# Token placement split between VectorE and GpSimd, first convolution taps moved to ScalarE and GpSimd, in a fused Mamba and mixture-of-experts layer

## The chip, the core and the metric

The kernel runs on one core of a Trainium2 chip. The time is that of one execution on the device, in microseconds (us); the median of several runs is given. A second figure is the span of one profiled execution, from its first to its last instruction.

The engines are called as in the profile: PE (TensorE, matmul; PEld is its weight load), DVE (VectorE), ACT (ScalarE), POOL (GpSimd), SP (SyncE, which issues most DMAs). Each has a queue of its own and works it off in order. They meet only at semaphores.

## What is computed

For x of shape 8 x 512 x 256 (batch, time, channels), with everything in float32:

```python
xn = layernorm(x)
# Mamba branch, per batch of 512 steps
x_ssm, x_gate = split(xn @ in_proj_w.T + in_proj_b)
x_conv = silu(causal_conv_4_taps(x_ssm) + conv_b)
B, C = split(x_conv @ bc_w.T + bc_b)            # 16 states
dt = softplus(x_conv @ dt_w.T + dt_b)
h = h * exp(dt * -exp(A_log)) + dt * B * x_conv   # over time, each channel and state
y = (sum over states of h * C + x_conv * D) * silu(x_gate)
mamba = layernorm(y @ out_w.T + out_b + xn) * ln_g + ln_b
# expert branch, on all 4096 tokens
logits = silu(xn @ rw1 + rb1) @ rw2 + rb2         # 8 experts, the best 2 are taken
w = softmax over the two taken logits
moe = xn + sum over the two of w * (silu(xn @ we1[e] + be1[e]) @ we2[e] + be2[e])
out = x + mamba + moe
```

## The kernel before

**Stage one** (to about 71 us) normalises x, transposes it, computes the router's logits and writes xn to scratch memory. **Stage two** begins with a block that runs once, and then has a loop over 8 batches of 9 steps. In each step PE computes one tile of 128 tokens through one expert (`up`, `down`), ACT applies Silu and the weights, POOL gathers a later tile's tokens and scatters this one's results with indirect DMAs, and DVE runs two of the 16 states of the Mamba scan: `times_b` (L947), `scan` (L954), `times_c` (L961). ACT makes the decay factors for the scan (`decay`, L778) and POOL adds up y (L598). A switch between Silu and Exp costs ACT a table load each time (L805). 71 steps carry an expert tile.

**The block that runs once** is what matters here. DVE first does the routing arithmetic (L1031 to L1081) on small tables of 128 x 256 and less, about 40 instructions, nearly each waiting for the one before (`link`): the best two experts of each token, and for each of the 2 x 4096 pairs a slot number, split in a tile number `af` (0 to 73) and a position `bf` in the tile. `idv` is the token id of a pair and `wv` its softmax weight. ACT gives an exponential for it (L883, waited for by L1079).

Then the ids and weights are **placed** in tables by matmul, in 8 chunks of 8 slots a lane each (`NCH`, `CH`). For a chunk:
- DVE makes a one-hot of the tile number, `oa` (one instruction, L1088, 8 x 74 elements a lane), and one of the position, `ob` (L1093, 8 x 128 elements).
- POOL multiplies oa by the ids (`ids_in`, L664), ACT multiplies it by the weights in 8 activations (`weights_in`, L795). The two halves form `ov`.
- PE adds ob^T x ov to the table in PSUM (`place`, L1307, 8 matmuls).

All is double-buffered: a chunk waits until the matmuls of the last but one are done (`s_placed`). The first batch's convolution stands between: ACT makes x_ssm and the first tap (`conv_in`, L697, L706), DVE adds the other three taps for each half of the channels (`tap`, L928, a fused multiply-add of 512 elements), three after chunk 1 and three after chunk 3. DVE also counts which expert each tile has (L1105 to L1108, `te_i`). PE does the matmuls for B, C and the step sizes (`first`, L1320) before chunk 4, ACT reads them (`first_bc`, `first_dt`), SP stores B and C, which are then loaded back once for each state, spread to all lanes (`rep`).

Last, DVE copies the placed table out of PSUM: `sid` (scatter ids), `wslot` (weights), `gid` (gather ids), L1115 to L1117. The gather of the first tile waits for that, then PE transposes it (`turn_x`, L1228), ACT copies it (`copy_x`, L785), and `up` begins. ACT meanwhile does exp and ln for the step size (L755, L759), the first decays and y's start (`start_sum`, L769). The **gate** projection of batch 0 (PE L1179, ACT L713) stands in steps 0 and 1 of the loop. SP loads the next batch's xn (`load_xnt`, L508) only when that projection has been done, and the loads of rep (L544) stand behind it in SP's queue.

## Time and profile before

| | |
|---|---|
| median of 3 runs | 923.11 us (922.67 to 924.55) |
| the profiled execution, its time | 921.83 us |
| the profiled execution, its span | 919.7 us |
| busy over the span | PE 85%, DVE 85%, ACT 72%, POOL 65% |
| mean granted TensorE clock | 0.962 of full speed |

The profile lists the busy time of each engine, groups of equal instructions with what ended the idle time before them, and the chain of work that ended last. A share of busy time is an average over very different stages, so the stretch from 71 to 160 us is read in its own timeline.

### The profile page before, as it was taken

To read this page: it belongs to the slowest core of one execution; us is meant where nothing else is said; L and a number is where in the kernel's file an instruction comes from. 1 tells how busy PE (TensorE), PEld (TensorE's weight loads), DVE (VectorE), ACT (ScalarE), POOL (GpSimd) and SP (SyncE) were. 2 spreads that over 40 slices of the span, in tenths; PEclk is the share of its full clock that TensorE was granted. 3 is DMA by queue.
4 is the path that set the end of the run, shared out by engine and by line. 5 is a ranking of instruction groups with operands and counts; after the bars stand their busy time and mean duration, and the time that the engine had idled before them with its cause. 6 is when DMAs were issued, how large, how long until landed. Compare 5 with 4: busy or idle time off the path is not lost.

```text
span 919.7 us, 14382 instructions
## 1 busy us (share of the span) xinstructions
PE 785.5 (85%) x4533; PEld 631.8 (69%) x4533; DVE 783.9 (85%) x774; ACT 663.4 (72%) x1134; POOL 599.1 (65%) x384
## 2 busy tenths in 40 slices
PE   3994959988999899898998899989889998999942
PEld 2661747867777778677876777677768776778831
DVE  6817947999989978997899889989899889989993
ACT  1433678878689768976897869887888778869920
POOL 3570425767577757776678847885688477758861
PEclk9995879999999999999999999999999999999986
DMA  9949536667577856787658866785678586977541
GB/s 286 390 167 294 200 144 230 200 202 244 189 238 209 253 191 226 208 260 238 223 184 247 275 182 213 224 286 172 222 212 276 180 256 196 265 226 235 186 91 24
DMA packets 81928, 201.02 MB, mean 219 GB/s; under 512 B 7936, under 2 KB 41216, under 8 KB 81728
## 3 DMA queue, kind: packets, MB, share of 16 engines
q1 hardware_dynamic: 61424, 171.46, 53.4%
q0 software_dynamic: 19168, 26.59, 15.2%
q10 hardware_dynamic: 1264, 2.05, 0.7%
q8 instruction: 40, 0.66, 0.3%
q14 instruction: 32, 0.26, 0.1%
HBM read 174.38 MB, written 26.61 MB: 219 GB/s over the span
## 4 chain that ended last, share of the span: by engine, by line
DVE 30%; PE 23%; ACT 14%; DMA 11%; issue 11%; POOL 3%; DVEq 0%; ACTq 0%; POOLq 0%; SPq 0%
DVE ps_drive L954 11%; PE ps_up L1248 9%; DVE ring L961 7%; DMA out<-yo,sid 6%; DVE ps_drive L947 6%; PE ps_yx L1262 5%; PE ps_fr L1179 4%; ACT L805 4%; ACT da L778 3%; DMA out<-xtok 3%; DVE xx L928 2%; DMA bc_scratch<-sp 1%; PE ps_fr L1204 1%; PE ps_up L1242 1%; POOL y L598 1%
## 5 line engine op out<-in xcount | busy, mean ns | idle before, releaser
L598 POOL TENSOR_TENSOR y<-y,ring 128x1024 f32<-128x1024 f32 x126 | 323.0, 2563 | 65.6 <-ACT y L769 52.5
L954 DVE TENSOR_TENSOR_SCAN ps_drive<-da,ps_drive 128x1024 f32<-128x1024 f32 x128 | 293.7, 2295 | 37.3 <-ACT da L778 33.6
L1248 PEld LDWEIGHTS ps_up<-xgt,w1s 128*128 128x128 f32 x2272 | 280.5, 194 | 18.2 <-issue 9.9
L1248 PE MATMUL ps_up<-xgt,w1s 128*128 128x128 f32 x2272 | 280.0, 277 | 0.0
L1262 PE MATMUL ps_yx<-w,ht 128*128 x1136 | 272.7, 384 | 0.0
L1262 PEld LDWEIGHTS ps_yx<-w,ht 128*128 128x128 f32 x1136 | 207.7, 193 | 29.2 <-issue 5.0
L587 POOL DMA_INDIRECT out<-yo,sid x71 | 116.4, 1639 | 128.3 <-ACT yo L820 99.2
L805 ACT ACT_TABLE_LOAD x143 | 183.5, 1283 | 2.5
L947 DVE TENSOR_TENSOR ps_drive<-ps_u,rep 128x1024 f32<-128x1024 f32 x128 | 157.3, 1229 | 25.0 <-DMA rep<-bc_scratch 16.2
L778 ACT ACTIVATE da<-gd,col 128x511 f32<-128x511 f32 x256 | 168.3, 710 | 0.0
L961 DVE TENSOR_TENSOR ring<-ps_drive,rep 128x1024 f32<-128x1024 f32 x128 | 156.6, 1223 | 3.9
L812 ACT ACTIVATE ht<-ps_up 128x512 f32<-128x512 f32 x142 | 80.7, 587 | 74.6 <-PE ps_up L1248 74.3
L1179 PE MATMUL ps_fr<-xx,wm 128*128 128x512 f32 (+1 forms) x212 | 104.9, 618 | 17.2 <-ACT sp L740 12.7
L578 POOL DMA_INDIRECT xg<-xn_scratch,gid x71 | 72.8, 1025 | 30.5 <-PE ps_up L1228 13.3
L1242 PE MATMUL ps_up<-sel,bpart 96*128 96x512 bf16 x142 | 55.3, 390 | 27.3 <-ACT xgt L785 26.1
L1179 PEld LDWEIGHTS ps_fr<-xx,wm 128*128 128x128 f32 (+1 forms) x212 | 35.5, 185 | 47.8 <-issue 32.2
L820 ACT ACTIVATE yo<-ps_yx,wslot 128x256 f32<-128x256 f32 x71 | 33.0, 464 | 40.5 <-DMA out<-yo,sid 31.5
L928 DVE SCALAR_TENSOR_TENSOR xx<-xs,col,xx 128x512 f32<-128x512 f32 x48 | 52.3, 1090 | 9.9 <-ACT xx L706 9.2
L1242 PEld LDWEIGHTS ps_up<-sel,bpart 96*128 x142 | 14.0, 99 | 55.3 <-issue 54.4
L1228 PE MATMUL ps_up<-ident,xg 128*128 128x128 f32 x142 | 27.9, 279 | 18.7 <-ACT ht L812 9.9
L1228 PEld LDWEIGHTS ps_up<-ident,xg 128*128 128x128 f32 x142 | 19.3, 142 | 28.3 <-issue 22.0
L237 POOL TENSOR_TENSOR w<-w,da 128x1024 f32<-128x1024 f32 x8 | 18.8, 2351 | 23.0 <-DVE da L288 14.1
(172 smaller groups left out, 710.5 us busy)
## 6 DMA issues: line engine op xcount, KB each, us to landing
w1s<-in_we SPq DMA_DIRECT2D x71, 1024.0 KB, 7.4
rep<-bc_scratch SPq DMA_DIRECT2D x128, 512.0 KB, 4.8
w<-in_we SPq DMA_DIRECT2D x8, 1024.0 KB, 12.0
w<-in_x SPq DMA_DIRECT2D x8, 512.0 KB, 11.2
xn_scratch<-da SPq DMA_DIRECT2D x8, 512.0 KB, 7.1
out<-w POOLq DMA_DIRECT2D x8, 512.0 KB, 6.5
xnt_scratch<-xx SPq DMA_DIRECT2D x8, 512.0 KB, 5.6
xx<-xnt_scratch SPq DMA_DIRECT2D x8, 512.0 KB, 3.2
```

What stands on the lines that cost most here:

```text
L587: pool.indirect_dma_start(out[:, :], bass.IndirectOffsetOnAxis(ap=sid[:, s:s + 1], axis=0), yo[:, :], None, bounds_check=TOK - 1, oob_is_e ...
L598: pool.tensor_tensor(y[:, :, :], y[:, :, :], ring[:, g % RING, :, :], ALU.add).then_inc(s_sum, 1)
L778: act.activation(da[:, g % DECAYS, k, 1:], dtt[:, k, 1:], ACT.Exp, scale=aneg[:, k, n:n + 1]).then_inc(s_decay, 1)
L805: act.activation(scrap[:, n % 4:n % 4 + 1], col[:, 0:1], func).then_inc(s_table, 1)
L812: act.activation(ht[:, j % HBUF, 4 * h:4 * h + 4, :], psum[f"up{h}"][:, :].rearrange("p (k c) -> p k c", c=P), ACT.Silu).then_inc(s_hidden, 1)
L947: dve.tensor_tensor(drive[:, :, :], u[:, :, :], rep[:, g % REPS, 0:1, :].to_broadcast([P, KD, L]), ALU.mult).then_inc(s_times_b, 1)
L954: dve.tensor_tensor_scan(states, da[:, g % DECAYS, :, :].rearrange("p k l -> p (k l)"), states, 0.0, ALU.mult, ALU.add).then_inc(s_scanned, 1)
L961: dve.tensor_tensor(ring[:, g % RING, :, :], drive[:, :, :], rep[:, g % REPS, 1:2, :].to_broadcast([P, KD, L]), ALU.mult).then_inc(s_times ...
L1179: mm = pe.matmul(psum["fr"][0:rows_out, :], wm[:, k, at:at + rows_out], src[:, k, :], start=(k == 0), stop=(k == KD - 1))
L1242: pe.matmul(bank[:, :], bup[:, bass.ds(e, 1), :], sel[:, 4 * h:4 * h + 4].unsqueeze(2).to_broadcast([PARTS, 4, P]), start=True, stop=False)
L1248: mm = pe.matmul(bank[:, c * P:(c + 1) * P], w1s[:, q, k, at:at + P], xgt[:, k, :], start=False, stop=(c == 3 and k == KD - 1))
L1262: mm = pe.matmul(yx_y, ht[:, j % HBUF, k, :], w2[:, bass.ds(e, 1), k, :], start=False, stop=(k == KH - 1))
```

## The change

- `oa` is gone. DVE writes the id half of ov directly: 8 instructions a chunk, each `(k_j == af) * idv` for one slot column (74 elements), then ob as before. POOL writes the weight half likewise with 8 instructions a chunk. ACT has no part in it any more. DVE and POOL no longer wait for each other, only for `s_placed`. Both buffers of ov now lie in `da`.
- First taps: ACT computes the six products (three per half, `products_of`), POOL adds them to xc (`first_taps`). DVE does all one-hots without taps between.
- The gate projection of batch 0 moves from the loop's steps 0 and 1 to just before the placements (PE) and behind the taps' products (ACT).
- PE's matmuls for B, C and step sizes move from before chunk 4 to behind the last chunk, and what ACT does with them with it. copy_x(0) moves ahead of ln_dt, and the first Silu of the experts ahead of the first decays. Three decays instead of two are made then.
- `gid` is written first, and the gather waits for it alone.

```diff
-        pair = [a.rearrange("p b k l -> p (b k l)") for a in (da[:, 0:2, :, :], gd[:, :, :, :])]
-        oa = [a[:, 2 * CH * MC:3 * CH * MC].rearrange("p (a c) -> p a c", c=MC) for a in pair]
-        ov = [a[:, 0:2 * CH * MC].rearrange("p (a v c) -> p a v c", v=2, c=MC) for a in pair]
+        placed = da.rearrange("p b k l -> p (b k l)")
+        ov = [placed[:, q * 2 * CH * MC:(q + 1) * 2 * CH * MC].rearrange("p (a v c) -> p a v c", v=2, c=MC)
+              for q in range(2)]
+        products = [a[:, k, :] for a in (ring[:, 2, :, :], ring[:, 3, :, :], da[:, 3, :, :]) for k in range(KD)]
...
-        uses = [("in", 0, 0), ("in", 0, 1)]
+        uses = [("in", 0, 0), ("in", 0, 1), ("gate", 0, 0), ("gate", 0, 1)]
...
                 def gather(j):
-                    pool.wait_ge(s_tables, 2)
+                    pool.wait_ge(s_tables, 1)
...
-                def ids_in(n):
+                def first_taps(m):
+                    pool.wait_ge(s_tap0, m + 1)
+                    for t in range(1, TAPS):
+                        if t > 1:
+                            pool.wait_ge(s_taps, (TAPS - 1) * m + t - 1)
+                        at = (TAPS - 1) * m + t
+                        pool.wait_ge(s_products, at)
+                        pool.tensor_tensor(xc[:, m, :], xc[:, m, :], products[at - 1], ALU.add).then_inc(s_taps, 1)
+
+                def weights_in(n):
                     q = n % 2
-                    pool.wait_ge(s_values, 1)
                     if n > 1:
                         pool.wait_ge(s_placed, n - 1)
-                    pool.wait_ge(s_tile_onehot, n + 1)
-                    pool.tensor_tensor(ov[q][:, :, 0, :], oa[q],
-                                       idv[:, bass.ts(n, CH)].unsqueeze(2).to_broadcast([P, CH, MC]),
-                                       ALU.mult).then_inc(s_ids_in, 1)
+                    for c in range(CH):
+                        at = n * CH + c
+                        ins = pool.tensor_scalar(ov[q][:, c, 1, :], k_j, af[:, at:at + 1], wv[:, at:at + 1],
+                                                 ALU.is_equal, ALU.mult)
+                    ins.then_inc(s_weights_in, 1)
...
-                    for c in range(CH):
-                        at = n * CH + c
-                        act.activation(ov[q][:, c, 1, :], oa[q][:, c, :], ACT.Copy,
-                                       scale=wv[:, at:at + 1]).then_inc(s_weights_in, 1)
...
+                def products_of(m):
+                    for t in range(1, TAPS):
+                        w = C_CW + TAPS * m + t
+                        act.activation(products[(TAPS - 1) * m + t - 1], xs[:, m, t:t + L], ACT.Copy,
+                                       scale=col[:, w:w + 1]).then_inc(s_products, 1)
...
-                for n in range(NCH):
-                    if n == 4:
-                        conv_act(0)
-                    if n == 5:
-                        first_bc()
-                    weights_in(n)
+                for m in range(KD):
+                    gate_in(0, m, front["gate", 0, m])
+                conv_act(0)
+                first_bc()
                 for m in range(KD):
                     first_dt(m)
                 exp_dt(0)
+                copy_x(0)
                 ln_dt(0)
-                copy_x(0)
-                table_of(ACT.Exp)
-                act.wait_ge(s_a, 2)
-                for r in range(NU):
-                    decay(0, 0, r)
-
-                start_sum(0)
                 table_of(ACT.Silu)
                 for h in range(2):
                     hidden(0, h)
                 copy_x(1)
                 table_of(ACT.Exp)
+                act.wait_ge(s_a, 2)
+                for r in range(NU):
+                    decay(0, 0, r)
+                decay(0, 1, 0)
+                start_sum(0)
...
                     if n > 1:
-                        dve.wait_ge(s_ids_in, n - 1)
-                        dve.wait_ge(s_weights_in, (n - 1) * CH)
-                    dve.tensor_tensor(oa[q], k_j.unsqueeze(1).to_broadcast([P, CH, MC]),
-                                      af[:, bass.ts(n, CH)].unsqueeze(2).to_broadcast([P, CH, MC]),
-                                      ALU.is_equal).then_inc(s_tile_onehot, 1)
-                    if n > 1:
                         dve.wait_ge(s_placed, n - 1)
+                    for c in range(CH):
+                        at = n * CH + c
+                        ins = dve.tensor_scalar(ov[q][:, c, 0, :], k_j, af[:, at:at + 1], idv[:, at:at + 1],
+                                                ALU.is_equal, ALU.mult)
+                    ins.then_inc(s_ids_in, 1)
...
-                for m in range(KD):
-                    for n in (2 * m, 2 * m + 1):
-                        one_hot(n)
-                    for t in range(1, TAPS):
-                        tap(0, m, t)
+                for n in range(3):
+                    one_hot(n)
...
                 proj_in(0, 1, 1)
+                for m in range(KD):
+                    proj_in(0, KD + m, front["gate", 0, m])
...
                 for n in range(NCH):
-                    if n == 4:
-                        pe.wait_ge(s_conv, KD)
-                        first(FIRST[0], W_BC, NBC)
-                        for m in range(KD):
-                            first(FIRST[m + 1], W_DT + m * P, P)
                     chunk(n)
+                pe.wait_ge(s_conv, KD)
+                first(FIRST[0], W_BC, NBC)
+                for m in range(KD):
+                    first(FIRST[m + 1], W_DT + m * P, P)
```

The queue of DVE at the start of the placements, before (`da` and `gd` hold oa and ov of the two buffers, `ring` holds ob, `rep` the small tables, `xx` the convolution):

```order
L1081 TENSOR_TENSOR rep<-rep 128x32 [waits s_link]
L1088 TENSOR_TENSOR da<-rep 128x592 [waits s_xn_stored1,s_xn_stored0]
L1093 TENSOR_TENSOR ring<-rep 128x1024
L1088 TENSOR_TENSOR gd<-rep 128x592
L1093 TENSOR_TENSOR ring<-rep 128x1024
L928 SCALAR_TENSOR_TENSOR xx<-xs,col,xx 128x512 [waits s_tap0]
L928 SCALAR_TENSOR_TENSOR xx<-xs,col,xx 128x512 [waits s_taps] x2
L1088 TENSOR_TENSOR da<-rep 128x592 [waits s_weights_in,s_ids_in]
L1093 TENSOR_TENSOR ring<-rep 128x1024 [waits s_placed]
```

and after the change (the line numbers are those of the changed kernel):

```order
L1089 TENSOR_TENSOR rep<-rep 128x32 [waits s_link]
L1097 TENSOR_SCALAR da<-rep 128x74 [waits s_xn_stored1,s_xn_stored0]
L1097 TENSOR_SCALAR da<-rep 128x74 x7
L1100 TENSOR_TENSOR ring<-rep 128x1024
L1097 TENSOR_SCALAR da<-rep 128x74 x8
L1100 TENSOR_TENSOR ring<-rep 128x1024
L1097 TENSOR_SCALAR da<-rep 128x74 [waits s_placed]
L1097 TENSOR_SCALAR da<-rep 128x74 x7
L1100 TENSOR_TENSOR ring<-rep 128x1024
```

Each wide oa became eight narrow instructions, the taps left this queue, and the only wait for another engine is the one for PE's earlier matmuls.

The queue of POOL at the same place, before (behind the branch comes stage two):

```order
L572 UNCONDITIONAL_BRANCH [waits barrier_Pool_Activation_PE_DVE_SP_gather]
L664 TENSOR_TENSOR da<-da,rep 128x8x74 [waits s_tile_onehot,s_values]
L664 TENSOR_TENSOR gd<-gd,rep 128x8x74 [waits s_tile_onehot,s_values]
L664 TENSOR_TENSOR da<-da,rep 128x8x74 [waits s_tile_onehot,s_placed,s_values]
L664 TENSOR_TENSOR gd<-gd,rep 128x8x74 [waits s_tile_onehot,s_placed,s_values]
```

and after:

```order
L573 UNCONDITIONAL_BRANCH [waits barrier_Pool_Activation_PE_DVE_SP_gather]
L666 TENSOR_TENSOR xx<-xx,ring 128x512 [waits s_products,s_tap0]
L666 TENSOR_TENSOR xx<-xx,ring 128x512 [waits s_products,s_taps] x2
L666 TENSOR_TENSOR xx<-xx,ring 128x512 [waits s_products,s_tap0]
L666 TENSOR_TENSOR xx<-xx,da 128x512 [waits s_products,s_taps] x2
L674 ISA
L674 TENSOR_SCALAR da<-rep 128x74 [waits s_values,s_xn_stored1,s_xn_stored0]
L674 TENSOR_SCALAR da<-rep 128x74 x15
L674 TENSOR_SCALAR da<-rep 128x74 [waits s_placed]
L674 TENSOR_SCALAR da<-rep 128x74 x7
```

Six additions now run while DVE is still at the routing arithmetic, and 64 short instructions stand where 8 wide ones stood.

## Rows read from the trace of the kernel before

**Rows 1.** The page: each engine's busy time, share of the span and instructions.

```profile
PE 785.5 (85%) x4533; PEld 631.8 (69%) x4533; DVE 783.9 (85%) x774; ACT 663.4 (72%) x1134; POOL 599.1 (65%) x384
```

**Rows 2.** The chain that ended last, in order: start, duration, engine and line.

```profile
81.97 0.18 DVE rep L1054
...
89.03 0.77 DVE da L1088
89.80 1.14 DVE ring L1093
90.94 1.66 DVE gd L1088
...
121.58 0.21 DVE gid L1117
...
184.77 1.23 DVE ps_drive L947
...
220.50 2.31 DVE ps_drive L954
```

**Rows 3.** Timeline of the placements: start, duration, engine, line, operation, [idle before].

```profile
89.95 2.02 POOL L664 TENSOR_TENSOR da<-da,rep 128x592 f32<-128x592 f32 x1 [23.57 <-DVE da L1088]
90.85 1.75 DVE L1088 TENSOR_TENSOR gd<-rep 128x592 f32<-128x592 f32 x1
...
92.12 4.28 PE L1307 MATMUL ps_up<-da,ring 128*128 128x148 f32 x16 [7.95 <-ACT da L795]
...
118.73 2.25 PE L1307 MATMUL ps_up<-gd,ring 128*128 128x148 f32 x16 [0.62 <-ACT gd L795]
```

**Rows 4.** Timeline of DVE and POOL near 46 us, from narrow windows.

```profile
45.71 1.05 DVE L288 TENSOR_SCALAR da<-w,sp 128x256 f32<-128x256 f32 x3
...
46.67 2.44 DVE L288 TENSOR_SCALAR da<-w,sp 128x256 f32<-128x256 f32 x1
...
46.59 2.38 POOL L237 TENSOR_TENSOR w<-w,da 128x1024 f32<-128x1024 f32 x1 [2.75 <-DVE da L288]
```

**Rows 5.** Groups of instructions: count | busy us, mean ns of one | idle before.

```profile
L257 POOL TENSOR_TENSOR w<-w,bpart 96x1024 f32<-96x1024 f32 x1 | 2.1, 2121 | 0.1
...
L609 POOL TENSOR_SCALAR mv<-mv 128x4 f32<-128x4 f32 x7 | 1.6, 224 | 0.6 <-issue 0.2
...
L256 POOL CAST bpart<-w 96x1024 bf16<-96x1024 f32 x1 | 1.0, 1033 | 0.1
...
L257 POOL TENSOR_TENSOR w<-w,bpart 96x256 f32<-96x256 f32 x1 | 0.7, 667 | 0.1
...
L256 POOL CAST bpart<-w 96x256 bf16<-96x256 f32 x1 | 0.4, 392 | 0.1
...
L769 ACT ACTIVATE y<-xx,col 128x512 f32<-128x512 f32 x16 | 10.6, 711 | 0.0
...
L928 DVE SCALAR_TENSOR_TENSOR xx<-xs,col,xx 128x512 f32<-128x512 f32 x48 | 52.3, 1090 | 9.9 <-ACT xx L706 9.2
```

**Rows 6.** Busy us of PE, PEld, DVE, ACT, POOL; PE clock, DMA share, GB/s.

```profile
71.40:89.00 17.60, 7.77 (x10) 2.53 (x10) 13.99 (x40) 4.63 (x7) 0.00 (x0) 0.60 1.00 325
```

**Rows 7.** Timeline behind the placements.

```profile
129.68 0.66 PE L1228 MATMUL ps_up<-ident,xg 128*128 128x128 f32 x2 [8.70 <-DMA xg<-xn_scratch,gid]
...
133.60 2.30 DVE L954 TENSOR_TENSOR_SCAN ps_drive<-da,ps_drive 128x1024 f32<-128x1024 f32 x1 [4.20 <-ACT da L778]
...
137.37 1.06 ACT L812 ACTIVATE ht<-ps_up 128x512 f32<-128x512 f32 x2
```

**Rows 8.** Timeline of the first steps, DVE and SP's queue.

```profile
148.79 2.30 DVE L954 TENSOR_TENSOR_SCAN ps_drive<-da,ps_drive 128x1024 f32<-128x1024 f32 x1 [0.45 <-ACT da L778]
...
152.51 0.96 SPq L544 DMA_DIRECT2D rep<-bc_scratch  x2
...
161.03 1.23 DVE L947 TENSOR_TENSOR ps_drive<-ps_u,rep 128x1024 f32<-128x1024 f32 x1 [3.76 <-DMA rep<-bc_scratch]
...
166.14 1.88 DVE L928 SCALAR_TENSOR_TENSOR xx<-xs,col,xx 128x512 f32<-128x512 f32 x1 [1.55 <-ACT xx L706]
```

More of the change, by code:

```diff
@@ L493, in build @@
                 uses.append(("out", b - 1, 1))
-            uses += [("gate", b, 0), ("gate", b, 1)]
+                uses += [("gate", b, 0), ("gate", b, 1)]
             if b < B - 1:
@@ L838, in step @@
                     prepare = b < B - 1
-                    if i + 1 < IN:
+                    if i + 1 < IN and s > 0:
                         decay(b, i + 1, 0)
@@ L846, in step @@
                             hidden(s + 1, h)
-                    if i in (0, 1):
+                    if i in (0, 1) and b > 0:
                         gate_in(b, i, front["gate", b, i])
@@ L1108, in _ @@
                 dve.tensor_scalar(te_i[:, :], wslot[:, :], -1.0, None, ALU.add).then_inc(s_expert, 1)
-                for n in range(4, NCH):
+                for n in range(3, NCH):
                     one_hot(n)
@@ L1114, in _ @@
                 dve.wait_ge(s_expert, 1)
+                dve.tensor_scalar(gid[:, :], ids, k_pad, float(TOK - 1), ALU.add, ALU.min).then_inc(s_tables, 1)
                 link(dve.tensor_scalar(sid[:, :], ids, k_pad, None, ALU.add))
                 dve.tensor_copy(wslot[:, :], psum["up0"][:, MC:2 * MC]).then_inc(s_tables, 1)
-                dve.tensor_scalar(gid[:, :], ids, k_pad, float(TOK - 1), ALU.add, ALU.min).then_inc(s_tables, 1)
                 for r in range(DECAYS):
@@ L1282, in step @@
                     e_after = expert(s + 2) if s + 2 < MT else None
-                    if i == 0:
+                    if i == 0 and b > 0:
                         proj_in(b, KD, front["gate", b, 0])
@@ L1291, in step @@
                         down(s, e, 1)
-                    if i == 0:
+                    if i == 0 and b > 0:
                         proj_in(b, KD + 1, front["gate", b, 1])
@@ L1312, in chunk @@
                     pe.wait_ge(s_ids_in, n + 1)
[L1313 removed]
+                    pe.wait_ge(s_weights_in, n + 1)
                     for a in range(CH):
@@ L1324, in _ @@
                 for n in range(NCH):
[L1325 to L1329 removed]
                     chunk(n)
+                pe.wait_ge(s_conv, KD)
+                first(FIRST[0], W_BC, NBC)
+                for m in range(KD):
+                    first(FIRST[m + 1], W_DT + m * P, P)
                 pe.wait_ge(s_first_read, 3)
+                pe.wait_ge(s_tables, 2)
                 turn_x(0)
[L1334 removed]
                 e = expert(0)
```

19 lines of the change are left out of this document (8 added, 11 removed).

## The prediction, made before the changed kernel ran

> **What bounds the kernel now.** I read the page first: no engine is the bound over the whole span, PE and DVE are both busy for 85% of it and ACT for 72% [rows 1]. The change leaves the loop over 71 expert steps as it was and rewrites what stands between the routing arithmetic and the first step, about 80 to 150 us. So I followed the chain of waits there. It runs on DVE through the routing arithmetic to 89.0 us, on through the one-hots and taps (L1088, L1093, L928), to the last placement matmuls, the table gid at 121.6 [rows 2], then the gather, a transpose and ACT's table loads and decays. What moves the end of this stage moves the kernel: from 184.8 to 222.8 the chain is DVE work with no gap, five steps of multiply, scan, multiply [rows 2]. A delay of VectorE by then is a delay of the end.
>
> Two marks serve for the sum: T, when the pair weights are ready and the one-hots start (89.03), and E, when the last placement matmul ends (118.73 + 2.25 = 120.98) [rows 3].
>
> The timeline of 89 to 93 us shows what paces the placements. The first oa of DVE takes 0.77 us, the next 1.75. POOL's multiply began at 89.95 and ended at 91.97; the second oa has 592 elements, 0.62 us at the pace of its neighbours (1024 elements in 1.14 us with the step to the next), and 91.97 + 0.62 is just its end, 92.60 [rows 2, 3]. So VectorE waited until GpSimd was through, and GpSimd (2.02 us for 1.30 us of work, below) had waited for ob before that. The two engines take turns at SBUF. One chunk then costs 2.80 us (89.80 to 92.60) [rows 2], and ACT's eight activations hide behind it.
>
> **Does that hold for a tensor_scalar?** It is the form that the change puts on both engines. At 46.67 an L288 (256 elements) started while POOL ran from 46.59 to 48.97; it took 2.44 us and ended at 49.11, 0.14 after POOL [rows 4]. Undisturbed, three take 1.05 us with 0.41 for the last one, so they start 0.32 apart [rows 4]. It does wait for GpSimd, and of its 0.32 us only 0.14 is streaming, 0.185 is fixed.
>
> The Trainium skill says the same of the port (SBUF — State Buffer, "Who interferes with whom": the pair is an exclusive lock, tensor_scalar can take it, and so does a VectorE instruction with two SBUF inputs against a reading GpSimd one); the traces agree. It speaks against this change, which puts both engines on short instructions of that kind.
>
> **Part 1, taps to ACT and POOL.** Removed from DVE: six L928, at their mean of 1.09 us (waits for POOL in it) 6.5 us of the chain [rows 5]. Added on ACT: six Copy with scale, 0.71 us each as L769 [rows 5], in a stretch where ACT is busy 4.63 of 17.6 us [rows 6]. The exp of the logit difference moves behind them, to about 87.9; DVE asks for it some 0.7 us before T, so nothing is lost there, the less if DVE is late.
> Added on POOL: six additions of 512 elements. POOL's two-input price is 667 ns for 256 and 2121 for 1024 elements, so 1.89 ns each on 0.18 fixed [rows 5]: 1.15 us each, 6.9 us, from the first product (81.5) to about 91. POOL was idle there (0.00 busy) [rows 6], but the routing chain of DVE was not: from 81.97 to 89.03 it is about twenty linked instructions, nearly all with two SBUF inputs or of the copy and tensor_scalar kind [rows 2]. I walked both queues against each other, each waiting for the other's running instruction: the links at L1054, L1056, L1060, both L1066 and the first cast are held for about 0.7, 1.2, 0.4, 1.0, 0.4 and 0.4 us; the two reductions and the links with a PSUM input pass. That is **T later by 4.0 us** (bounds 0, if such short instructions slip between, and 6.9, every addition in full).
>
> **Part 2, the placements.** VectorE: eight TENSOR_SCALAR of 74 elements in place of one oa. By the above 0.185 + 0.04 = 0.23 us apart [rows 4], 1.84 a chunk, plus 1.14 for ob: 2.98. (Bounds 0.04, streaming alone, and 0.32, the 256-element step.) GpSimd: 224 ns for four elements (L609), plus 70 elements at 0.83 ns (the casts, 1033 and 392 ns) gives 0.28 us, 2.26 a chunk [rows 5]. No row has a compare with column operands on GpSimd: bounds 0.22, that row alone, and 0.45, twice its fixed part. While ob streams, POOL's reads are held [rows 3], so its chunk is 2.26 + 1.14 = 3.40, and DVE's eight, taking turns with POOL's eight, come to the same. I take **3.40 us a chunk**, against 2.80 now (bounds 2.25, PE's own chunk [rows 3], and 5.2 = 8 x (0.23 + 0.28) + 1.14 if nothing overlaps).
>
> The Trainium skill has another price for VectorE (VectorE: DVE Perf Modes, the section on the TRN2 errata: 58 cycles plus the elements over the speed-up, at 0.96 GHz). An estimate from that page is 0.10 us for each of the eight and 1.93 us a chunk, below PE's; by it the sum below would end about 9 us lower (8 x (3.40 - 2.25), since PE then sets the pace), if GpSimd kept up.
>
> PE: the two gate projections now stand before chunk 0. They take the clock of that stretch (0.60) [rows 6], 3.6 us each with ACT's Silu table and the first gate between, until about 93.6; ob(0) is ready at 96.4, so they are covered. Their cover is thin only if T doesn't move. Chunk 0 takes 4.1 us at the low clock (the row's 4.28 laps over into the next) [rows 3], placed at 100.5, while DVE, which no longer has taps to fill with, wants buffer 0 at 99.8: 0.7 us of wait. The expert table (L1105 to L1108) stays, 1.74 us.
> Sum: T = 89.03 + 4.0 = 93.0; + 8 x 3.40 = 27.2; + 0.7 + 1.7; + 2.25 for the last chunk: E = 124.9. **Against 120.98 that is 3.9 later.**
>
> **Part 3, behind E.** The matmuls for B, C and the step sizes (5.7 us) come after the chunks, so do their ACT reads, the store of B and C, exp and ln. On SP the bc store now precedes the rep loads directly. gid first saves 0.5 us of the gather, which is covered: ACT is at exp_dt until E + 9.2, and only then copies x, at E + 9.6 (now E + 9.4, behind the transpose) [rows 7]. Then ln (with its table), Silu table, hidden(0), copy_x(1), Exp table, decays. PE has worked until E + 5.6 instead of idling 8.70 us [rows 7], so I take the first up at the high clock, hidden(0) done at E + 15 instead of E + 17.45 (138.43) [rows 7]. The first scan then starts at E + 18.1, now E + 12.6 [rows 7]: **VectorE is 5.5 us later there**. But behind it three waits stood: 0.45 for a decay, 3.76 for a rep transfer, 1.55 for the next conv_in [rows 8]. The second comes from SP: load_xnt waits for the second gate projection of step 1, and rep, issued at 152.51, queues behind it [rows 8]. With the gates early, that is gone. PE loses 2 x 1.9 us of projections in step 0 and is about 2 us ahead at step 3. So VectorE ends up 5.5 - 5.8 = **0.4 earlier** (the other end: cold PE, scan at E + 20.2, 1.6 later).
>
> **Sum:** 3.9 - 0.4 = +3.5. The profiled execution would have 919.7 + 3.5 = 923.2 span and 925.3 time. The median of the runs shown is 1.3 above the profiled time: **926.6 us**.
>
> **Rivals.**
> (a) The port doesn't bite: each instruction holds it so briefly (0.04 of 0.23 us) that both streams slip through. T stays, chunks take 2.98: chunk 0 waits for the gates until 93.6 and is placed at 97.7; 97.7 + 3.0 + 1.7 + 14.9 + 2.25 = 119.6, 1.4 earlier, with the tail 1.8: 921.3. At PE's pace of 2.25 a chunk: 97.7 + 2.25 + 1.7 + 11.25 + 2.25 = 115.2, 916.9. For it: POOL's start at 46.59 fell between two instructions of DVE and cost POOL nothing visible (2.38 us for 1024 elements, by the price above 2.12) [rows 4, 5]. Against it: the 0.62 and 0.14 behind POOL's end. It wins as long as T stays and a chunk is under 3.3 us (97.7 + 6 x 3.3 + 1.7 + 2.25 = 121.4 is today's E plus what the tail gives). Chance 0.26.
> (b) GpSimd's compare is slow, or nothing overlaps. At 0.40 us each, 8 x 0.40 + 1.14 = 4.34 a chunk: 93 + 34.7 + 1 + 2.25 = 131, 933. Fully serial 5.2: 93 + 41.6 + 1.7 + 2.25 = 138.6, +17.2, 940. It passes the forecast once an instruction on GpSimd costs over 0.33. For it: two column operands and a compare, seen in no row. Chance 0.17.
> (c) The start's shift is swallowed by later waits in the loop (of the kind of the 1.55 for conv_in) [rows 8]: 923.1. Against it: the gapless DVE chain from 184.8. Chance 0.07.
> The forecast's own case, 3.1 to 3.8 us a chunk with T 3 to 6 later, gives E 0.8 to 8.7 later and 923.5 to 931. Chance 0.50.
>
> **How the numbers follow.** A measurement of this kernel can tell about 0.2%, 1.8 us, from no change. (a) is faster but for its slow edge; (c) and the low edge of the forecast are the same; the rest is slower: faster 0.25, same 0.14, slower 0.61. The range leaves out the fast end of (a) and the serial end of (b): 918 to 937; the forecast alone has 923.5 to 931.
>
> **What the profile after would show.** Right: DVE's routing links at 82 to 91 us longer than 0.42, T near 93; one-hots 3.4 us apart with ob blocking POOL; E near 125; first scan 18 us behind E; no rep wait near 160. Wrong, to the fast side: links still 0.17 to 0.42 and T near 89, or VectorE's eight in under 1.2 us. Wrong, to the slow side: GpSimd's instruction over 0.35 us, PE waiting for the weights before each chunk. If E is as forecast but the end is not, the tail is what I mis-sized.

## The result, and the profile after

The changed kernel takes 950.11 us (median of 6 runs, 945.89 to 951.33), the kernel before 923.43 (6 runs beside it, 920.87 to 925.20): a ratio of 1.0282, 95% interval 1.0254 to 1.0310. I had forecast 926.6 with a range of 918 to 937. The sign was right, the size was not: the loss is 26.7 us where I had 3.5, and the range ended 13 us too early. Here and below a median is over all runs of a kernel, while a ratio leaves out the few runs that lie over 1.5% above the fastest of their kernel.

The page of the profiled execution (949.45 us, span 947.7), the rows that answer [rows 1] and three groups of instructions:

```profile
PE 798.2 (84%) x4533; PEld 640.2 (68%) x4533; DVE 790.4 (83%) x824; ACT 649.0 (68%) x1074; POOL 641.5 (68%) x446
...
DVE 28%; PE 20%; ACT 16%; DMA 11%; issue 9%; POOL 7%; SPq 0%; DVEq 0%; ACTq 0%; POOLq 0%
...
L674 POOL TENSOR_SCALAR da<-rep 128x74 f32<-128x74 f32 x64 | 48.3, 773 | 3.4 <-DVE rep L1089 3.4
L1313 PE MATMUL ps_up<-da,ring 128*128 128x148 f32 x128 | 26.3, 380 | 26.3 <-POOL da L674 26.3
```

POOL is 42 us busier than before, and 48.3 of its microseconds are the 64 instructions that make the pair weights, 773 ns each. My sum had 280 for one by itself and 425 with VectorE's wide compare spread over the eight of a chunk (3.40 / 8). POOL's share of the chain that ended last is 7%, where it was 3%. PE's last column says the rest: in all 26.3 us of its waits within the placements it waited for POOL, and for nobody else.

The timeline of the stage, POOL first, then PE, then DVE (start, duration, engine, line, operation, [idle before and its releaser]). These rows stand against [rows 2, 3]:

```profile
79.72 5.27 POOL L666 TENSOR_TENSOR xx<-xx,ring 128x512 f32<-128x512 f32 x4 [14.19 <-ACT ring L886]
85.07 2.74 POOL L666 TENSOR_TENSOR xx<-xx,da 128x512 f32<-128x512 f32 x2
91.18 48.27 POOL L674 TENSOR_SCALAR da<-rep 128x74 f32<-128x74 f32 x64 [3.37 <-DVE rep L1089]
```

```profile
86.29 3.48 PE L1183 MATMUL ps_fr<-xx,wm 128*128 128x512 f32 x4 [2.88 <-ACT gd L727]
98.17 4.29 PE L1313 MATMUL ps_up<-da,ring 128*128 128x148 f32 x16 [8.40 <-POOL da L674]
...
134.84 4.29 PE L1313 MATMUL ps_up<-da,ring 128*128 128x148 f32 x16 [5.29 <-POOL da L674]
139.60 2.71 PE L1313 MATMUL ps_up<-da,ring 128*128 128x148 f32 x16 [0.47 <-POOL da L674]
```

```profile
79.87 1.40 DVE L1064 TENSOR_TENSOR ht<-rep 128x256 f32<-128x256 f32 x1
...
81.90 0.54 DVE L1068 TENSOR_TENSOR_SCAN rep<-rep 128x8 f32<-128x8 f32 x1
...
82.67 1.13 DVE L1070 TENSOR_SCALAR rep<-rep 128x8 f32<-128x8 f32 x1
...
84.29 0.98 DVE L1072 TENSOR_TENSOR xtok<-xtok,rep 128x256 f32<-128x256 f32 x1
85.31 1.37 DVE L1074 TENSOR_TENSOR ht<-y,xtok 128x256 f32<-128x256 f32 x1
...
87.34 0.75 DVE L1074 TENSOR_TENSOR ht<-xtok 128x256 f32<-128x256 f32 x1
...
90.87 1.93 DVE L1097 TENSOR_SCALAR da<-rep 128x74 f32<-128x74 f32 x8
92.72 1.26 DVE L1100 TENSOR_TENSOR ring<-rep 128x1024 f32<-128x1024 f32 x1
...
102.50 2.03 DVE L1097 TENSOR_SCALAR da<-rep 128x74 f32<-128x74 f32 x8 [5.56 <-PE ps_up L1313]
```

How to read them. POOL's third row is one unbroken stretch: from 91.18 to 139.45 it never waits, 48.27 / 8 = 6.03 us a chunk. Everything else in the stage waits for it: PE before every chunk, DVE for a buffer that PE could not free (5.56 us at 102.50). DVE's eight narrow instructions take 1.93 us, 0.23 apart, as forecast. Before that stretch, six routing links stand out: 1.40, 0.54, 1.13, 0.98, 1.37 and 0.75 us. They lie beside POOL's six additions (79.72 to 87.81). The same six in the kernel before:

```profile
82.18 0.42 DVE L1056 TENSOR_TENSOR ht<-rep 128x256 f32<-128x256 f32 x1
...
83.22 0.17 DVE L1060 TENSOR_TENSOR_SCAN rep<-rep 128x8 f32<-128x8 f32 x1
...
83.63 0.17 DVE L1062 TENSOR_SCALAR rep<-rep 128x8 f32<-128x8 f32 x1
...
84.29 0.43 DVE L1064 TENSOR_TENSOR xtok<-xtok,rep 128x256 f32<-128x256 f32 x1
84.75 0.42 DVE L1066 TENSOR_TENSOR ht<-y,xtok 128x256 f32<-128x256 f32 x1
...
85.84 0.43 DVE L1066 TENSOR_TENSOR ht<-xtok 128x256 f32<-128x256 f32 x1
```

The stage by marks. S is where stage two starts (the memset of xs: 71.45 before, 69.13 after; stage one is the same code, and its 2.3 us are spread). T is the start of the first one-hot, E the end of the last placement matmul (139.60 + 2.71 = 142.31).

| | before | after | difference |
|---|---|---|---|
| S | 71.45 | 69.13 | -2.3 |
| S to T | 17.58 | 21.74 | +4.2 |
| T to E | 31.95 | 51.44 | +19.5 |
| E to the end of the span | 798.7 | 805.4 | +6.7 |
| span | 919.7 | 947.7 | +28.0 |

### The profile page after: what moved, and what is told of

The parts are those of the page before. It is cut to its first block, busy times and chain, and to the rows that moved or that the text cites. A ratio compares the mean times of both kernels' runs of the same rounds, so it can differ in the third digit from the quotient of the medians.

```text
span 947.7 us, 14419 instructions
## 1 busy us (share of the span) xinstructions
PE 798.2 (84%) x4533; PEld 640.2 (68%) x4533; DVE 790.4 (83%) x824; ACT 649.0 (68%) x1074; POOL 641.5 (68%) x446
## 4 chain that ended last, share of the span: by engine, by line
DVE 28%; PE 20%; ACT 16%; DMA 11%; issue 9%; POOL 7%; SPq 0%; DVEq 0%; ACTq 0%; POOLq 0%
DVE ps_drive L962 11%; DMA out<-yo,sid 8%; PE ps_up L1252 7%; DVE ring L969 6%; DVE ps_drive L955 6%; POOL da L674 5%; ACT L808 4%; PE ps_fr L1183 4%; ACT da L792 3%; PE ps_yx L1266 3%; PE ps_fr L1208 2%; DMA bc_scratch<-sp 2%; DVE xx L936 1%; DMA rep<-bc_scratch 1%; ACT ht L815 1%
## 5 line engine op out<-in xcount | busy, mean ns | idle before, releaser
L1252 PEld LDWEIGHTS ps_up<-xgt,w1s 128*128 128x128 f32 x2272 | 283.9, 196 | 17.7 <-issue 9.4
L1252 PE MATMUL ps_up<-xgt,w1s 128*128 128x128 f32 x2272 | 283.5, 279 | 0.0
L1183 PE MATMUL ps_fr<-xx,wm 128*128 128x512 f32 (+1 forms) x212 | 108.5, 636 | 25.4 <-ACT sp L754 16.6
L936 DVE SCALAR_TENSOR_TENSOR xx<-xs,col,xx 128x512 f32<-128x512 f32 x42 | 44.8, 1068 | 8.6 <-ACT xx L720 8.1
L674 POOL TENSOR_SCALAR da<-rep 128x74 f32<-128x74 f32 x64 | 48.3, 773 | 3.4 <-DVE rep L1089 3.4
L1313 PE MATMUL ps_up<-da,ring 128*128 128x148 f32 x128 | 26.3, 380 | 26.3 <-POOL da L674 26.3
L1313 PEld LDWEIGHTS ps_up<-da,ring 128*128 128x128 f32 x128 | 24.3, 265 | 29.3 <-issue 29.3
```

The lines of the kernel that those rows point to most:

```text
L674: ins = pool.tensor_scalar(ov[q][:, c, 1, :], k_j, af[:, at:at + 1], wv[:, at:at + 1], ALU.is_equal, ALU.mult)
L1183: mm = pe.matmul(psum["fr"][0:rows_out, :], wm[:, k, at:at + rows_out], src[:, k, :], start=(k == 0), stop=(k == KD - 1))
L1252: mm = pe.matmul(bank[:, c * P:(c + 1) * P], w1s[:, q, k, at:at + P], xgt[:, k, :], start=False, stop=(c == 3 and k == KD - 1))
```

## The experiments

Each ratio is to runs of the kernel before that were taken beside the run; their medians are 923.4 to 924.3 us.

**The disputed cost by itself.** To the end of the kernel before I added a row of instructions on POOL that write tiles nobody reads any more: the form of the change, and the same with one property taken away at a time; then the form again beside VectorE's narrow and wide ones.

```diff
+for r in range(6):
+    pool.tensor_scalar(spot(MC), src, c1, c2, ALU.is_equal, ALU.mult)   # then mult, mult; constants; 8 and 592 elements
+for r in range(8):                          # once beside 24 narrow ones on VectorE, once beside 4 wide compares
+    ins = pool.tensor_scalar(spot(MC), src, c1, c2, ALU.is_equal, ALU.mult)
```

> The kernel before, with a tail of instructions on idle engines that write unused tiles (the output isn't touched). GpSimd alone, 74 elements a lane: six tensor_scalar with is_equal and mult by columns, six mult and mult by columns, six is_equal and mult by constants, six mult and mult by constants, six with one mult by a constant, six with is_equal and mult by columns on 8 elements, two of them on 592. Then eight of the first form with VectorE working at 24 tensor_scalar of 74, and eight with VectorE working at 4 is_equal of 1024 elements (two SBUF inputs). Theory P (price): the form itself costs about 0.60 us on idle GpSimd, and mult by constants about 0.28, so the price sits in the columns or in the compare; 592 elements would then be about 1.0. Theory L (turns at the port): alone the form costs 0.28, and 0.6 to 0.77 only with VectorE beside it. Both: beside the wide VectorE instruction an instruction of GpSimd takes 1.4 to 1.5, since that one holds the port for 1.1 us.

The timeline of POOL and DVE there:

```profile
922.91 3.63 POOL L701 TENSOR_SCALAR ring<-gam,col 128x74 f32<-128x74 f32 x6 [4.09 <-DMA out<-xtok]
926.53 2.36 POOL L703 TENSOR_SCALAR ring<-gam,col 128x74 f32<-128x74 f32 x6
928.87 2.60 POOL L705 TENSOR_SCALAR ring<-gam 128x74 f32<-128x74 f32 x6
931.43 1.36 POOL L707 TENSOR_SCALAR ring<-gam 128x74 f32<-128x74 f32 x6
...
934.96 2.32 POOL L711 TENSOR_SCALAR ring<-gam,col 128x8 f32<-128x8 f32 x6
937.27 4.66 POOL L713 TENSOR_SCALAR ring<-da,col 128x592 f32<-128x592 f32 x2
...
942.64 5.38 POOL L718 TENSOR_SCALAR ring<-gam,col 128x74 f32<-128x74 f32 x8
942.58 5.58 DVE L1217 TENSOR_SCALAR xx<-gam,col 128x74 f32<-128x74 f32 x24 [26.81 <-POOL da L715]
...
949.04 8.67 POOL L725 TENSOR_SCALAR ring<-gam,col 128x74 f32<-128x74 f32 x8
948.98 2.36 DVE L1222 TENSOR_TENSOR gd<-gam 128x1024 f32<-128x1024 f32 x2 [0.82 <-POOL da L722]
```

Divide each row by its count. Compare and multiply by two columns (L701): 0.604 us. Without the compare (L703): 0.393. With constants in place of columns (L705): 0.433. With neither (L707): 0.227, somewhat less than my estimate of 0.28. So the columns cost 0.17 and the compare 0.21, and neither was in my price. Between 8 and 74 elements (0.387 and 0.604) the form goes by 3.3 ns an element, and two of 592 took 2.33 us each, where I had expected about 1.0. Beside 24 narrow instructions of VectorE it takes 5.38 / 8 = 0.67, 0.07 more; beside four wide compares 8.67 us for eight, (8.67 - 8 x 0.604) / 4 = 0.96 us for each wide one. VectorE itself lost nothing beside it: 5.58 / 24 = 0.23, and 1.22 us for a wide compare.

That makes the stage: 64 x 0.604 = 38.7, plus 8 x 0.96 = 7.7 for the eight wide compares of ob, is 46.3 of the 48.27 us. The other 1.9 us is of the size of the turns beside the narrow ones (64 x 0.07 would be 4.5 if all stood beside one). The changed kernel's own trace has the same price. At 95.89 VectorE runs ob, from 98.60 it is idle; the last line, of another view, is for all 64 (shortest, median and longest in ns):

```profile
95.89 1.54 POOL L674 TENSOR_SCALAR da<-rep 128x74 f32<-128x74 f32 x1
...
98.60 2.40 POOL L674 TENSOR_SCALAR da<-rep 128x74 f32<-128x74 f32 x4
...
L674 POOL TENSOR_SCALAR da<-rep x64: 611/615/2157, 91.2 to 138.8; 128x74 f32<-128x74 f32 x64
```

With nothing beside it an instruction takes 2.40 / 4 = 0.60 us; the one beside ob takes 0.9 more. The longest, 2.16 us, stood beside ob and the compare of the expert table behind it.

**The change in its parts.** First everything but the placements; then the taps alone; then the rest of the tail alone.

```diff
 # everything but the placements (e2): as after, but ids and weights as before
-ins = pool.tensor_scalar(ov[q][:, c, 1, :], k_j, af[:, at:at + 1], wv[:, at:at + 1], ALU.is_equal, ALU.mult)
+pool.tensor_tensor(ov[q][:, :, 0, :], oa[q], idv[:, bass.ts(n, CH)]..., ALU.mult)      # and ScalarE's eight weights
```

> The changed kernel with the placements as before: wide one-hot on VectorE, one wide multiply on GpSimd, eight activations on ScalarE; taps, gates ahead and the matmuls behind stay as changed. Theory P: the placements carry 20 to 25 us of the 26.7, the chunks go back to 2.8 us, E to about 3 to 5 later than before by the taps' 4.1, the time to 926 to 931. Theory L gives the same here. A rival, that the loss sits in the order behind the placements (cold clock of TensorE, decays late), leaves over 10 us: 935 or more.

> The kernel before, with the first taps alone moved to ScalarE and GpSimd; all else as before. Port theory: the routing arithmetic on VectorE ends 4.1 us later (the six additions hold the port), and the six fused taps, 6.2 us between the chunks, are gone from VectorE; the chunks are then paced by turns at the port, 2.8 each: E about 1 earlier to 1 later, time 921 to 925. If the port doesn't matter for the arithmetic, T stays and the time is 918 to 920.

> The kernel before, with the order around the placements alone changed: first gate projections ahead, matmuls for B, C and step sizes behind the last chunk, their ScalarE work with it, gid first; both buffers of the one-hots in one tile. My prediction's step: E 2 earlier or equal (the six matmuls, 5.7 us, leave the middle, where they stood before chunk 4), the first scan at E + 18 to 20 instead of E + 12.6, no wait for rep near 160: 0.4 earlier to 1.6 later behind E, time 920 to 925. If the late first scan isn't absorbed by the missing waits, 926 to 930.

Everything but the placements: 925.35 us, ratio 0.9993 (0.9961 to 1.0025). Taps alone: 925.73, 1.0012 (0.9983 to 1.0041). Gates ahead, B, C and step sizes behind: 927.43, 1.0037 (1.0011 to 1.0063). From the ratio 0.9993 to 1.0282 is 2.9%, about 26.7 us, with some 3 us of doubt: **the placements carry the whole loss** within that. The other two parts together can't be told from no change, though the tail alone costs 0.37%, clear of noise by little. The first one-hot of the three, in this order (S at 70.24, 69.22 and 68.74):

```profile
91.58 0.77 DVE L1111 TENSOR_TENSOR da<-rep 128x592 f32<-128x592 f32 x1
```

```profile
90.57 0.77 DVE L1109 TENSOR_TENSOR da<-rep 128x592 f32<-128x592 f32 x1
```

```profile
86.13 0.77 DVE L1087 TENSOR_TENSOR da<-rep 128x592 f32<-128x592 f32 x1
```

S to T is 21.34 and 21.35 with the taps moved and 17.39 without: the shift of T is the taps' doing, and theirs alone. E I had placed wrongly in two of the three. With everything but the placements it was to come 3 to 5 us later, and it stands 49.3 us behind S as in the kernel before (49.5); with the taps alone it was to move by 1 us at most, and it stands 51.4 us behind S, 1.9 later.

**All on VectorE.** The changed kernel with the weights taken from POOL and given to VectorE too: 16 narrow instructions and ob a chunk on one engine.

```diff
+for c in range(CH):
+    ins = dve.tensor_scalar(ov[q][:, c, 1, :], k_j, af[:, at:at + 1], wv[:, at:at + 1], ALU.is_equal, ALU.mult)
-for n in range(NCH):
-    weights_in(n)          # GpSimd
```

> The changed kernel with GpSimd out of the placements: VectorE makes the ids and the weights, 16 narrow instructions (74 elements, compare and multiply) and one wide compare (ob) a chunk. Theory: the change lost its 24 us to GpSimd's own price of the narrow form, 0.604 us against VectorE's 0.23. Then a chunk is 16 x 0.23 + 1.14 = 4.8 us instead of about 6.3, the last placement matmul ends about 43 us behind the moment the weights are ready (51.4 in the changed kernel), and the kernel takes about 941 us, though one engine now does all the work of two. Rival: it is the number of narrow instructions and their waits, whichever engine has them; then taking them all on one engine makes it longer still: chunk 1.93 (measured for eight) + 8 x 0.6, 6.7 us or more, 953 us or above.

```profile
91.14 1.92 DVE L1081 TENSOR_SCALAR da<-rep 128x74 f32<-128x74 f32 x8
92.97 1.92 DVE L1086 TENSOR_SCALAR da<-rep 128x74 f32<-128x74 f32 x8
94.80 1.23 DVE L1089 TENSOR_TENSOR ring<-rep 128x1024 f32<-128x1024 f32 x1
95.93 1.92 DVE L1081 TENSOR_SCALAR da<-rep 128x74 f32<-128x74 f32 x8
...
131.33 3.82 PE L1302 MATMUL ps_up<-da,ring 128*128 128x148 f32 x16 [1.54 <-DVE ring L1089]
```

A chunk is 95.93 - 91.14 = 4.79 us, T to E 44.0 (91.14 to 135.15) against 51.4. One engine does the narrow work of two in less time than the two did. The whole-kernel times scatter: 940.04 to 950.21 in four runs, median 946.94, ratio 1.0252 (1.0195 to 1.0309); the profiled run is the 940.04. The stage agrees with the theory. The median is only 3 us below the changed kernel's where I had expected 9, and the two intervals overlap, so the times of the whole kernel show no sure gain; where the rest went I can't say from one profile.

**The compare alone.** The changed kernel with POOL's compare replaced by a multiply. It leaves out the selection of the weights, so its output is wrong; gathers and scatters go by the ids, which are as they were.

```diff
-ALU.is_equal, ALU.mult)    # GpSimd, the weights
+ALU.mult, ALU.mult)
```

> The changed kernel with GpSimd's compare replaced by a multiply, same columns, same count and places; so the weights half of the table is not the reference's, and gathers, experts and scatters go by the ids half, which is untouched. The probe gave 0.604 us with the compare and 0.393 without. Theory (each of the 64 instructions at its own price paces the stage): 64 x 0.211 = 13.5 us less between the weights' readiness and the last placement matmul (38 us instead of 51.4), 936 to 937 us. Rival (the stage is paced by something else that GpSimd's records only reflect, the turns with VectorE at the memory): little changes, 947 us or more.

```profile
L674 POOL TENSOR_SCALAR da<-rep 128x74 f32<-128x74 f32 x64 | 36.8, 589 | 5.8 <-DVE rep L1089 3.4 <-PE ps_up L1313 2.4
```

The group falls from 48.3 to 36.8 us, T to E from 51.4 to 41.9 (90.95 to 132.88), the kernel to 939.59 us, ratio 1.0143 (1.0088 to 1.0199). The form of one instruction, at the same place and count, moves the end by 10 us. The rival (POOL's records only reflect something else) falls. It is less than the 13.5 us I had worked out: each instruction became 0.18 us cheaper in the mean and not 0.21, and POOL now waits 2.4 us for buffers, which PE frees.

**POOL out, ScalarE back.** The changed kernel with the weights made on ScalarE from VectorE's ids.

```diff
+act.activation(ov[q][:, c, 1, :], ov[q][:, c, 0, :], ACT.Copy, scale=rw[:, at:at + 1])   # rw = weight / id
```

> The changed kernel with the weights on ScalarE, as before the change, but made from the ids (scale = weight over id), and GpSimd out of the placements. VectorE keeps the changed form: eight narrow instructions and ob, measured at 1.93 a chunk for the eight. Theory (all of the loss is GpSimd's narrow form): a chunk is 1.84 + 1.14 = 3.0 us, eight of them and the expert table 25.7, so the last placement matmul ends about 28 to 30 us behind the weights' readiness instead of 51.4, and the kernel takes 926 to 928 us, what the other parts of the change alone cost (925 to 927). Rival (VectorE's own narrow form costs too): a chunk of 3.5 or more, 931 us or more.

T to E is 32.9 us (91.46 to 124.33), not the 28 to 30 I had expected, but 18.6 less than in the changed kernel; 931.33 us, ratio 1.0071 (1.0036 to 1.0105). Its timeline has ACT's eight at 2.08 us starting only when DVE's eight are done, and DVE waiting 2.56 and twice 0.54 us for a buffer: ids, weights and matmul of one chunk now stand in a row, and two buffers don't cover that. The time is the one that I had given to the rival, VectorE's own narrow form costing too, and in part that is so. Its eight take 1.91 us where the wide compare took 0.77. The run named everything but the placements, which differs from this one only in how ids and weights are made, has T to E at 27.9 us, 4.9 less.

**The ids on VectorE.** The kernel before with the one multiply of POOL moved to VectorE.

```diff
-pool.tensor_tensor(ov[q][:, :, 0, :], oa[q], idv[:, bass.ts(n, CH)]..., ALU.mult).then_inc(s_ids_in, 1)
+dve.wait_ge(s_tile_onehot, n + 1)          # behind ob(n)
+dve.tensor_tensor(ov[q][:, :, 0, :], oa[q], idv[:, bass.ts(n, CH)]..., ALU.mult).then_inc(s_ids_in, 1)
```

> The kernel before with one thing moved: the multiply that makes the ids (592 elements) goes from GpSimd to VectorE, behind ob; ScalarE keeps the weights. If the 2.80 us of a chunk in the kernel before was turns at the memory between VectorE's two-input instructions and GpSimd's multiply, a chunk on VectorE is now 0.62 + 1.14 + 0.62 = 2.4 us, no longer than that with all of the work on one engine, and the last placement matmul ends 2 to 3 us earlier: 920 to 922 us, ratio 0.997 to 0.999. If not (the engines did not hold each other up and the chunk was set by PE or ScalarE), VectorE has 0.6 us more a chunk: 3.4 us, 927 to 929 us.

```profile
86.83 0.77 DVE L1074 TENSOR_TENSOR da<-rep 128x592 f32<-128x592 f32 x1
87.52 1.22 DVE L1079 TENSOR_TENSOR ring<-rep 128x1024 f32<-128x1024 f32 x1
88.65 0.77 DVE L1083 TENSOR_TENSOR da<-da,rep 128x592 f32<-128x592 f32 x1
89.34 0.77 DVE L1074 TENSOR_TENSOR gd<-rep 128x592 f32<-128x592 f32 x1
```

VectorE does a third instruction more and is done sooner: 2.51 us a chunk (86.83 to 89.34) against 2.80 in [rows 2], and the second oa takes 0.77 us where [rows 3] has 1.75. T to E is 30.6 against 31.95, 1.35 us less where I had expected 2 to 3; 920.12 us, ratio 0.9965 (0.9929 to 1.0000). That is the reading of [rows 3] borne out: two-input work on both engines takes turns.

**The tail in its halves.** Gates ahead alone, and B, C and step sizes behind alone. The second has ScalarE's order of the changed kernel with it (copy_x ahead of ln, Silu ahead of the decays).

```diff
 # e8: gates ahead only (PE, and ScalarE's gate_in with it)
+for m in range(KD):
+    proj_in(0, KD + m, front["gate", 0, m])        # before the first chunk
 # e12: B, C, step sizes behind only
-if n == 4:
-    pe.wait_ge(s_conv, KD)
-    first(FIRST[0], W_BC, NBC)                     # and first(...) of the step sizes
+first(FIRST[0], W_BC, NBC)                         # behind the loop over the chunks
```

> The kernel before with one piece of the change: batch 0's two gate projections and their activations ahead of the placements; B, C and the step sizes stay where they were. My prediction's tail: the wait for a rep transfer near 160 us (3.8 us) goes, because SP no longer stands behind the second gate projection of step 1, and PE loses 2 x 1.9 us in step 0. Theory (those waits were paid): span behind the last placement matmul 2 to 5.8 us shorter than the 798.7 of before, kernel 918.5 to 922. Rival (VectorE's waits there are slack that a later wait takes back): rep wait gone, span behind E within 1 us of before, 923 to 925 us.

> The complement: the kernel before with the matmuls and activations for B, C and the step sizes behind the placements, and ScalarE's order of ln, tables and decays as in the changed kernel; no gates ahead, taps and placements as before. Theory: the last placement matmul ends up to 5.7 us earlier if PE sets E there, less if VectorE does (the other runs say about 1 us); the first scan starts 19 to 20 us behind E instead of 12.6, so 6 us later against start, and nothing gives it back: 926 to 930 us. Rival (what I predicted: the later scan finds shorter waits behind it, and the sum is about zero): 923 to 925 us.

Gates ahead: 921.35 us, ratio 0.9975 (0.9949 to 1.0000). Firsts behind: 928.64, 1.0048 (1.0015 to 1.0081). The first scan of each, e8 then e12:

```profile
132.81 2.30 DVE L957 TENSOR_TENSOR_SCAN ps_drive<-da,ps_drive 128x1024 f32<-128x1024 f32 x1 [4.39 <-ACT da L779]
```

```profile
139.28 2.30 DVE L951 TENSOR_TENSOR_SCAN ps_drive<-da,ps_drive 128x1024 f32<-128x1024 f32 x1 [4.79 <-ACT da L778]
```

E is at 120.00 and 118.72, so the scan starts at E + 12.8 with the gates alone and at E + 20.6 with B, C and step sizes behind (E + 12.6 before, E + 20.2 after). E itself gained only 0.2 us against S from taking 5.7 us of matmuls out from between the chunks (E - S is 49.53 before, 49.30 here): VectorE set E, not PE.

With the gates ahead the wait for rep near 160 is gone, as I had expected, and batch 1 starts 99.8 us behind E instead of 103.0. The span behind E is 799.2 us all the same, against 798.7, where I had expected 2 to 5.8 less: in the profile the gain is taken back later. The medians have 2 us of it, and the interval of the ratio reaches 1.

**Two versions more.** Ids on VectorE with the gates ahead, and with the taps moved.

> All placement products but the weights on VectorE (ids multiply off GpSimd, as in the run before this one that took 920.1 us), and batch 0's gate projections ahead of the placements. If the gates alone are worth something, it adds: 916 to 919 us. If not, 919 to 922 us.

> The ids multiply on VectorE, and the first taps as in the change (six products on ScalarE, six additions on GpSimd). GpSimd then has no work in the placements, but its additions still meet VectorE's routing arithmetic. Theory (the additions move the readiness of the weights 4 us and nothing of it comes back unless VectorE sets the end of the placements): weights ready 21.3 us behind the stage's start instead of 17.4; VectorE saves 4.6 us of taps, but PE needs about 28.7 us from there with a cold first chunk and the 5.7 us for B, C and step sizes, so the last placement matmul ends at start + 50, 2 us later than without the taps moved: 922 us. Rival (VectorE sets the end): start + 47, 919 us.

With the gates ahead: **919.44 us, ratio 0.9956 (0.9932 to 0.9980)**, the lowest median of all, and faster than both kernels. It isn't told from the version with the ids alone (920.12), so the gates may add nothing to it. With the taps moved: 925.58, 1.0023 (0.9997 to 1.0049), where I had expected 922 or, by the rival, 919. There S to T is 21.65 and T to E 29.5: VectorE's six taps are gone from the placements and only 1.1 us of E comes back, since PE now runs there almost without a pause, for 4.3 us given up before T (21.65 against 17.37 with the ids alone). The taps belong where they were.

## Why the prediction was wrong, point by point

**What bounds it.** Right: the stage moves the end. 23.65 us more from S to E became 26.7 in the median.

**Part 1, T later by 4.0 us.** It was 4.2 (21.74 against 17.58), and the six held links make 4.1 of it. Four of the six that I had named were held (L1056, L1060 and both L1066, by 0.98, 0.37, 0.95 and 0.32 us, for my 1.2, 0.4, 1.0 and 0.4); the other two went free, and L1062 and L1064 were held in their place (0.96 and 0.55). POOL's additions took 1.32 us each in the first row (5.27 / 4) where I had 1.15. The run with the taps alone has 3.8; in it the copy and the first cast were held (1.00 in place of 0.17 and 0.52 in place of 0.20 us). So which links are held changes with the moment at which POOL's additions start, and 4.1 for my 4.1 is a sum of other terms than mine, in part luck. The rival that short instructions slip between falls for two-input work of POOL against two-input, tensor_scalar and copy work of DVE.

**Part 2, VectorE's eight.** Right in size: 0.23 us apart, 1.93 for eight. Wrong in mechanism: I had them take turns with POOL's eight, each engine waiting for the other. They hardly wait: 1.92 us for eight with POOL idle (all on VectorE), 1.90 to 2.10 with POOL at work in the changed kernel, and 0.23 each in the probe beside POOL.

**Part 2, POOL's eight: the step that failed.** I took 0.28 us for one and bounded it at 0.22 and 0.45, "twice its fixed part", though I had written that no row showed a compare with columns on GpSimd. It takes 0.604 alone. Worked through: my chunk of 3.40 becomes 8 x 0.604 = 4.83, plus 0.96 for ob, plus 0.24 of turns, 6.03 us. Eight chunks of 2.63 us more are 21.0 us; the 2.4 us that I had for the gates' wait and the expert table vanish, as they lie beside a POOL that never stops; POOL's late start and PE's last chunk add 0.3 and 0.5, T 0.2. That is 19.6, and from S to E I was short by 19.7 (73.18 against the 53.45 that E = 124.9 meant). The upper bound was no bound: it was a factor of two on a four-element row with other operands, and what a compare and columns add stood in none of its parts. The dearest pace that [rows 5] has, two-input work at 1.89 ns an element, would have made 0.32 us for 74 elements; so no row of before leads to 0.60, and the honest end lay further off. With 64 in a row on one engine, 0.1 us on each is 6.4 us of the kernel: that product, not the nearness of a row, should have set the width. And the rival (b) was right as a mechanism and stopped at 0.40 us for the same reason. That ob holds POOL for about its own length (1.14 in my sum, 0.96 measured) was right.

The Trainium skill (SBUF — State Buffer, "Who interferes with whom") has the port pair as an exclusive lock that tensor_scalar can take. The trace agrees for POOL's additions and DVE's links (1.37 against 0.42 us), and for POOL beside ob (0.96 us for each). For narrow tensor_scalar on both engines it hardly shows: 0.07 us on POOL, nothing on DVE.

**Part 3, the tail.** I had the first scan at E + 18.1 with E + 20.2 as the other end; it was E + 20.2. My own terms were added a little wrong: 5.5 - 5.8 is 0.3 earlier, not 0.4, and the other end is 7.6 - 5.8 = 1.8 later, not 1.6. Of the three waits behind the scan one of 0.46 us is left, as I had said. The first instruction of batch 1, before and after:

```profile
223.97 1.22 DVE L936 SCALAR_TENSOR_TENSOR gd<-xs,sp 128x1024 f32<-128x1024 f32 x1
```

```profile
248.02 1.22 DVE L944 SCALAR_TENSOR_TENSOR gd<-xs,sp 128x1024 f32<-128x1024 f32 x1
```

They stand 103.0 and 105.7 us behind E: of the 7.6 us by which the scan was later, 4.9 were given back by then, for my 5.8. From there to the end another 4.0 us were lost (699.7 against 695.7), in code that no kernel here changes.

I compared that second stretch in twelve profiles. The probe is left out, which has a tail of its own, and so is the version with ids on VectorE and gates ahead, whose profiled execution took 927.2 us against a median of 919.4. The seven with the firsts behind take 701.1 us on average (697.5 to 705.2), the five others 697.7 (695.7 to 699.5). PE is busy for 618 us against 613, and its granted clock there is 0.96 to 0.97 against 0.97 to 0.98. With one profile a kernel and ranges that overlap, this is a hint and no proof. By the timed runs the firsts behind cost 0.48% (4.4 us), the gates ahead give 0.25% (2.3 us), and both together cost 0.37% (3.4 us). So by them and by the changed kernel (26.7 less 23.65) the term was about +3 where I had -0.4. The run with everything but the placements says otherwise: E behind S as before, the same tail, and a ratio of 0.9993, some 3 us either way. The size of the term is open between these, and so is whether the lower clock is a cause of the loss or goes along with it; no run here tells it.

**The rivals.** (a), faster because nothing takes turns, was right for the narrow ones against each other (0.07 us) and wrong for ob and for T, and it fell on POOL's price in any case. (b) was the case, at a price outside its own span. (c) did not show: of the shift nothing was swallowed.

## What to carry to other kernels

Before work is given to an idle engine, find the price of that very form there: operation, kind of scalar operands and width. Here the form costs 0.604 us on GpSimd and 0.23 on VectorE, and all of my arguing about turns weighed less than that one number. If no row shows it, multiply the doubt on one instruction by their number, and let that set the range.

The weights of before cost next to nothing: ScalarE's eight activations ended together with POOL's multiply (89.89 + 2.08 and 89.95 + 2.02, both 91.97), while VectorE went on. Moving hidden work to the place where it is on the path buys nothing even at a fair price. And when two engines take turns, giving the second engine's part to the first can be the faster way, as the ids multiply showed in its stage (T to E 1.35 us shorter).

## What the runs showed of the hardware

- GpSimd's tensor_scalar, 74 elements: 0.227 us with two constants and no compare; columns add 0.17, the compare 0.21; on 592 elements 2.33 us. One multiply by a constant alone took 0.368 us (2.21 / 6), longer than two operations with constants.
- VectorE's tensor_scalar of 74 elements with two columns and a compare: 0.23 us apart, and 1.90 to 2.10 us for eight with GpSimd at work against 1.92 without.
- A wide two-input compare on VectorE (1024 elements, 1.22 us) costs GpSimd's tensor_scalar 0.96 us of standing still and VectorE nothing, also where GpSimd's instruction had begun first (at 128.43 in the changed kernel, ob at 128.73, which took 1.21 us); against GpSimd's own two-input instructions VectorE is held too (1.75 in place of 0.77 us for 592 elements).
- PE's chunk (8 matmuls of the program, 16 in the records) took 4.29 us where PE had idled 4.9 to 8.4 us before it and 2.25 to 2.28 behind waits of 0.47 to 1.84 us (the changed kernel, all but its last chunk, 2.71, and the third, 3.92 behind 4.41). The granted clock was 0.50, the lower level of 1.2 GHz, from 98.17 to 102.46, and 1.00, the upper one of 2.4 GHz, from 127.31 to 129.56. Here it cost 0.5 us, in the last chunk alone, since POOL set the pace of all others.
